# Dilation: the rows of the tiles m pitched like those of u

## The chip, the cores and the metric

The kernel runs on one core of a Trainium2 chip. The metric is the time of one execution on the device, in microseconds (us); lower is better.

## The reference

The input x is (8, 32, 256, 256) in float32. Two residual steps follow each other, each on a group-normalised x (16 groups of 2 channels):

```
x = x + dilation(_gn(x), kernel)           # 11 x 11 taps, R = 5
x = x + deformed(_gn(x), proj, dw, bn, off)   # projection, 3x3 depthwise, norm, gelu, offsets, bilinear sample

dilation: acc = -1e30
          for di, dj in 11 x 11:  acc = max(acc, pad[di:di+H, dj:dj+W] - kflat[channel, di*11+dj])
```

The change lies in the first step, the dilation: 121 taps, each a shifted copy of the image minus a constant of the channel, and the running maximum over all of them.

## The kernel before, in words

128 partitions hold 4 images x 32 channels, so there are two groups g of 128 planes. The program has four stages on one core: statistics and tables (to about 200 us), the dilation (to about 8.8 ms), the convolution and the resampling.

**Windows and chunks.** The dilation goes through each group in 16 windows of 16 output rows (WIN), and each window in 2 chunks of CR = 8 rows: 64 chunks in all. `u[s]` (two of them) is the window of x with a border of 5, 26 rows of UC = 266 elements; `dx[s]`, of the same shape, is the horizontal difference of neighbours in u, made by GpSimd (line 181). A tap pair (base, outer) needs max(u[base] - k1, u[outer] - k2), which is written as u[base] plus a relu of dx plus a constant.

**Four routes for the taps of a chunk.**

- m route, 22 pairs (`pool_pairs`): for 16 of them ScalarE writes relu(dx + gap) into `m[j % 4]` (line 591), for the other 6 (CLAMPED) GpSimd does so with a min/max (line 488). Then GpSimd adds u onto m in place (line 500; line 496 where the pair was clamped, with u as its first operand). VectorE takes acc_a = max(acc_a, m - k) (line 688; line 685 for the first of a chunk). acc_a is in PSUM.
- t route, 16 pairs (`dma_pairs`): ScalarE writes the relu into `t[j % 4]`, a DMA that GpSimd issues adds u onto t (line 471), VectorE takes the maximum (line 688). The rows of t have a pitch of 266.
- singles, 9 taps: VectorE reads u itself (line 688).
- chains: TensorE adds dx or u onto a PSUM tile (line 559), ScalarE applies a relu in place (line 609), VectorE merges a finished half chain into acc_b (line 662).

At the end of a chunk VectorE joins acc_a and acc_b (line 695) and writes x1 (line 701).

**Order.** Each engine works through an order written out by hand and repeated in every chunk. GpSimd's is `POOL_ORDER = "iitcitttcitittittcitdititcittiicttditittictitt"`: t is an add of the m route (t0 to t21), i the issue of a t-route DMA (i0 to i15), c a clamp, d a piece of dx for the next window. A writer of `m[j % 4]` waits until VectorE has used the pair four places earlier (`a_free`); four buffers are all there are.

**Layout.** `m[s]` is a tile of 8 rows of W + 4 = 260 elements (1040 bytes) of which 256 are used; the operand of u in an add is 8 rows of 256 elements at a pitch of 266 elements (1064 bytes), from row k*8 + di and column base. In the program before, tiles lie one behind the other in the on-chip memory, each at a multiple of 32 bytes: u0 begins at 23616, u1 at 51296, m0 at 139456, m1 at 147776, m2 at 156096, m3 at 164416, and the t tiles, acc_b and x1 follow them. So u0 and all m are at multiples of 64 bytes, u1 is 32 beyond one. The taps of the m route are, as (di, base): t0 (6,1), t1 (6,8), t2 (7,5), t3 (7,3), t4 (7,6), t5 (7,1), t6 (7,8), t7 (8,5), t8 (8,3), t9 (8,6), t10 (8,1), t11 (8,8), t12 (9,5), t13 (9,3), t14 (9,6), t15 (9,1), t16 (9,8), t17 (10,5), t18 (10,3), t19 (10,6), t20 (10,1), t21 (10,8).

**Other adds of GpSimd with two inputs**, which the prediction compares with: line 962, tap_a += tap_b, and line 968, h += tap_a, contiguous tiles of 4096 elements per partition, whose beginnings are 16384, 32768 or 49152 bytes apart; line 1290, dv = y[row + 1] - y[row], both operands in one tile of pitch 257; lines 1287, 1294 and 181, differences of neighbours, both operands in one tile and one element apart.

Of the kernel before, what the change touches and what calls it, by code (L numbers as in the profile page):

```python
# [15 lines left out]
P = 128  # L16
# [9 lines left out]
UR, UC = WR + 2 * R, W + 2 * R  # L26
CR = 8
# [27 lines left out]
MP, TP = 4, 4  # L55
# [57 lines left out]
def build(nc, x, params, proj_w, basis_in, mats_in, out):  # L113
# [5 lines left out]
    with ExitStack() as ctx:  # L119
# [21 lines left out]
        with ExitStack() as windows:  # L141

            u = [windows.enter_context(nc.sbuf_tensor(f"u{s}", [P, UR, UC], F32)) for s in range(2)]
            dx = [windows.enter_context(nc.sbuf_tensor(f"dx{s}", [P, UR, UC], F32)) for s in range(2)]
            outside = windows.enter_context(nc.sbuf_tensor("outside", [P, R, W], F32))
            win_loaded = [windows.enter_context(nc.semaphore(f"win_loaded{s}")) for s in range(2)]
            dx_ready = windows.enter_context(nc.semaphore("dx_ready"))
            stats_and_tables(nc, x_pl, params, basis_in, mats_in, mats, par, kt, nkt, gap_r, gap_l,
                             shift1, eps, small, pair_mean, u, dx, outside, win_loaded, dx_ready)
            dilation(nc, x_pl, x1_pl, ident, kt, nkt, gap_r, gap_l, rstd, shift1, sums1,  # L150
                     u, dx, outside, win_loaded, dx_ready)
# [182 lines left out]
def dilation(nc, x_pl, x1_pl, ident, kt, nkt, gap_r, gap_l, rstd, shift1, sums1,  # L334
# [31 lines left out]
    with ExitStack() as ctx:  # L366
        def sb(name, shape):
            return ctx.enter_context(nc.sbuf_tensor(name, shape, F32))
# [2 lines left out]
            return ctx.enter_context(nc.semaphore(name))  # L371


        m = [sb(f"m{s}", [P, CR, W + 4])[:, :, 0:W] for s in range(MP)]
        t = [sb(f"t{s}", [P, CR, UC]) for s in range(TP)]
        acc_b = sb("acc_b", [P, CR, W])
        x1 = sb("x1", [P, CR, W])
# [1070 lines left out]
```

## Time and profile before

| | |
|---|---|
| time, median of 3 | 10515.83 us (10509.91 to 10517.41) |
| the profiled execution's own time | 10515.12 us |
| its span | 10513.3 us |
| busy, of the span | VectorE 95%, GpSimd 90%, ScalarE 88%, TensorE 83% |
| DMA queue of GpSimd (q0) | 59.6% of the 16 engines |

The page of the profile gives the busy time of each engine, the span in 40 slices, and the costliest groups of instructions by line. A group's mean for GpSimd takes in the time in which an instruction lies in the engine's queue behind a DMA issue, so for its adds the distance from one start to the next says what one costs.

### The profile page before, as it was taken

Reading aid. Unit: us, or ns where it says so; the run is one execution under the profiler, and the core shown is the slowest. Engines: PE = TensorE matmul, PEld = TensorE weight load, DVE = VectorE, ACT = ScalarE, POOL = GpSimd, SP = SyncE. Lnnn points to the kernel's source line nnn. Section 1 sums busy time; section 2 is a strip of 40 time slices with the busy share of each in tenths; the row PEclk is TensorE's granted clock in tenths of the full one; section 3 lists DMA queues with packets and bytes.
Section 4 is the critical chain, followed back from the end, with each engine's and each line's share of the span. In section 5 each row is a group of like instructions: output and inputs, shape, how many; then the busy total and the mean of one; then the engine's idle time right before and its main releaser. Section 6 shows DMA issues by size and latency. Waiting matters only on the chain. (4 is left out here: it accounts for less than half of the span.)

```text
span 10513.3 us, 74673 instructions
## 1 busy us (share of the span) xinstructions
PE 8674.1 (83%) x18068; PEld 3359.2 (32%) x18068; DVE 10028.2 (95%) x5623; ACT 9204.1 (88%) x6861; POOL 9425.7 (90%) x3274
## 2 busy tenths in 40 slices
PE   2888888888888888888888888888888887888898
PEld 0333333333333333333333333333333333333333
DVE  8999999999999999999999999999999998998999
ACT  2999999999999999999999999999999996777776
POOL 2999999999999999999999999999999996666999
PEclk9999999999999999999999999999999998999999
DMA  8887878787878788888787888787888874433776
GB/s 316 156 158 152 158 149 157 149 156 152 157 154 158 155 158 155 153 157 157 155 157 154 156 156 157 154 157 155 156 157 157 156 139 130 166 155 140 267 280 252
DMA packets 442132, 1751.83 MB, mean 167 GB/s; under 512 B 23888, under 2 KB 130384, under 8 KB 392784
## 3 DMA queue, kind: packets, MB, share of 16 engines
q0 software_dynamic: 278528, 1110.51, 59.6%
q1 hardware_dynamic: 163152, 636.41, 16.0%
q8 instruction: 147, 2.41, 0.1%
q14 instruction: 305, 2.50, 0.1%
HBM read 391.58 MB, written 201.33 MB: 56 GB/s over the span
## 5 line engine op out<-in xcount | busy, mean ns | idle before, releaser
L559 PE MATMUL chain<-dx,mats 128*128 128x512 f32 x10240 | 5013.7, 635 | 971.4 <-ACT chain L609 970.3
L500 POOL TENSOR_TENSOR m<-m,u 128x2048 f32<-128x2048 f32 x1024 | 4783.9, 4835 | 21.6 <-ACT m L591 21.3
L688 DVE SCALAR_TENSOR_TENSOR acc_a<-m,kt,acc_a 128x2048 f32<-128x2048 f32 x1344 | 3162.9, 2353 | 70.7 <-POOL m L496 21.2
L559 PEld LDWEIGHTS chain<-dx,mats 128*128 128x128 f32 x10240 | 1927.3, 198 | 4057.6 <-ACT chain L609 2129.2
L609 ACT ACTIVATE chain<-chain,gap_r 128x1024 f32<-128x1024 f32 x2560 | 2696.4, 1087 | 245.4 <-PE chain L559 242.3
L688 DVE SCALAR_TENSOR_TENSOR acc_a<-t,kt,acc_a 128x2048 f32<-128x2048 f32 x1024 | 2411.9, 2355 | 34.2
L471 POOL DMA_DIRECT2D t<-u x1024 | 1621.1, 1695 | 450.6 <-ACT t L591 391.9
L496 POOL TENSOR_TENSOR m<-u,m 128x2048 f32<-128x2048 f32 x384 | 1891.1, 4925 | 0.0
L591 ACT ACTIVATE t<-dx,gap_l 128x2048 f32<-128x2048 f32 x768 | 1540.8, 2006 | 0.0
L559 PE MATMUL chain<-u,mats 128*128 128x512 f32 x3072 | 1456.0, 605 | 74.4 <-ACT chain L609 74.4
L688 DVE SCALAR_TENSOR_TENSOR acc_a<-u,kt,acc_a 128x2048 f32<-128x2048 f32 x576 | 1357.0, 2356 | 20.5
L591 ACT ACTIVATE m<-dx,gap_l 128x2048 f32<-128x2048 f32 x640 | 1281.7, 2003 | 23.2 <-DVE acc_a L688 23.2
L662 DVE SCALAR_TENSOR_TENSOR acc_b<-chain,kt,acc_b 128x1024 f32<-128x1024 f32 x768 | 965.8, 1279 | 66.2 <-PE chain L559 65.2
L559 PE MATMUL chain<-dx,neg_ident 128*128 128x512 f32 x1536 | 752.8, 627 | 330.9 <-ACT chain L609 330.9
L488 POOL TENSOR_SCALAR m<-dx,gap_l 128x2048 f32<-128x2048 f32 x384 | 966.2, 2516 | 28.3 <-DVE acc_a L688 28.2
L609 ACT ACTIVATE chain<-dx,gap_r 128x1024 f32<-128x1024 f32 x640 | 712.7, 1121 | 288.0 <-DVE acc_b L662 275.0
L559 PEld LDWEIGHTS chain<-u,mats 128*128 128x128 f32 x3072 | 547.2, 188 | 952.4 <-issue 557.2
L591 ACT ACTIVATE m<-dx,gap_r 128x2048 f32<-128x2048 f32 x384 | 766.6, 1996 | 0.0
L1054 DVE SCALAR_TENSOR_TENSOR hp<-o,par,hp 128x1024 f32<-128x1024 f32 x512 | 659.8, 1289 | 80.0 <-PE hp L868 66.5
L868 PE MATMUL hp<-o,diag 128*128 128x512 f32 x1024 | 528.5, 664 | 128.9 <-DVE h L1054 128.9
L591 ACT ACTIVATE t<-dx,gap_r 128x2048 f32<-128x2048 f32 x256 | 515.9, 2015 | 30.7 <-issue 16.4
L559 PEld LDWEIGHTS chain<-dx,neg_ident 128*128 128x128 f32 x1536 | 277.8, 194 | 805.9 <-ACT chain L609 544.4
(145 smaller groups left out, 6968.0 us busy)
## 6 DMA issues: line engine op xcount, KB each, us to landing
t<-u POOLq DMA_DIRECT2D x1024, 1059.0 KB, 8.8
u<-x_dram SPq DMA_DIRECT2D x32, 2688.0 KB, 26.7
xw<-x_scratch SPq DMA_DIRECT2D x62, 1152.0 KB, 7.3
xt<-x_dram SPq DMA_DIRECT2D x32, 2048.0 KB, 14.4
x_scratch<-x SPq DMA_DIRECT2D x64, 1024.0 KB, 11.1
h_scratch<-h SPq DMA_DIRECT2D x32, 2048.0 KB, 7.3
hw<-h_scratch SPq DMA_DIRECT2D x64, 1024.0 KB, 9.3
out_dram<-res SPq DMA_DIRECT2D x64, 1024.0 KB, 4.9
```

The lines of the kernel that those rows point to most:

```text
L471: nc.gpsimd.dma_start(t[j % TP][:].rearrange("p r w -> p (r w)")[:, 0:RUN], u[s][:].rearrange("p r w -> p (r w)")[:, first:first + RUN], a ...
L488: nc.gpsimd.tensor_scalar(m[j % MP], dx[s][:, top:top + CR, lo:lo + W], high, low, ALU.min, ALU.max).then_inc(m_clamped, 1)
L496: nc.gpsimd.tensor_tensor(m[j % MP], rows, m[j % MP], ALU.add if outer > base else ALU.subtract).then_inc(m_ready, 1)
L500: nc.gpsimd.tensor_tensor(m[j % MP], m[j % MP], rows, ALU.add).then_inc(m_ready, 1)
L559: added = nc.tensor.matmul(chain[h][:, r:r + 2, :], weight, src[:, top:top + 2, dj:dj + W], start=False, stop=True, skip_group_check=True)
L591: return nc.scalar.activation(dst, dx[s][:, k * CR + di:k * CR + di + CR, lo:lo + W], ACT.Relu, bias=gap[:, g, col(di, base):col(di, base) ...
L609: nc.scalar.activation(chain[h][:], src, ACT.Relu, bias=gap[:, g, col(di, base):col(di, base) + 1], scale=scale).then_inc(chain_relu[h], 1)
L662: nc.vector.scalar_tensor_tensor(out=part, in0=chain[h][:], scalar=kt[:, g, base:base + 1], in1=part, op0=ALU.subtract, op1=ALU.max).then_ ...
L688: nc.vector.scalar_tensor_tensor(out=acc_a[:], in0=src, scalar=k_base, in1=acc_a[:], op0=ALU.subtract, op1=ALU.max).then_inc(a_done, 1)
L868: last = nc.tensor.matmul(hp[q % 2][:, r:r + 2, :], diag[:, t, :], o[s][:, top:top + 2, tx:tx + W], start=(t == 0), stop=(t == TAPS_PE - 1))
L1054: nc.vector.scalar_tensor_tensor(out=out, in0=o[s][:, q * QR + ty:(q + 1) * QR + ty, tx:tx + W], scalar=par[:, COL_DW + t:COL_DW + t + 1], ...
```

## The change

Each m tile gets rows of UC = 266 elements in place of 260; still only the first 256 of a row are used. No instruction is added, removed or moved, and no wait changes. A tile grows from 8320 to 8512 bytes per partition, so m1, m2 and m3 begin 192, 384 and 576 bytes later, and the t tiles, acc_b, x1 and neg_ident 768 bytes later.

```
-        m = [sb(f"m{s}", [P, CR, W + 4])[:, :, 0:W] for s in range(MP)]
+        m = [sb(f"m{s}", [P, CR, UC])[:, :, 0:W] for s in range(MP)]
```

## Rows read from the trace of the kernel before

**Rows 1.** Page, part 1: busy us, share of the span, instructions of each engine

```profile
PE 8674.1 (83%) x18068; PEld 3359.2 (32%) x18068; DVE 10028.2 (95%) x5623; ACT 9204.1 (88%) x6861; POOL 9425.7 (90%) x3274
```

**Rows 2.** Busy time in 200 to 8700 us, the dilation

```profile
core 0: us, PE busy (x) PEld busy (x) DVE busy (x) ACT busy (x) POOL busy (x), PEclk, DMA share, GB/s
200.00:8700.00 8500.00, 7133.01 (x14728) 2729.63 (x14728) 8191.29 (x3930) 7898.89 (x5907) 8022.09 (x2921) 0.96 0.80 155
```

**Rows 3.** Waits of VectorE, 200 to 8700 us: total us, times, longest

```profile
DVE acc_a L685 <- issue: 72.2, 14, 5.3
DVE acc_b L662 <- PE chain L559: 64.2, 149, 5.8
DVE acc_a L688 <- POOL m L496: 20.8, 41, 1.2
DVE acc_a L685 <- POOL m L500: 20.0, 1, 20.0
DVE acc_a L688 <- POOL m L500: 19.0, 43, 0.5
```

**Rows 4.** Timeline of GpSimd over a chunk's end: start, duration, instruction, [idle before]

```profile
4346.97 1.21 POOL L471 DMA_DIRECT2D t<-u  x1 [0.44 <-issue]
4347.77 4.65 POOL L496 TENSOR_TENSOR m<-u,m 128x2048 f32<-128x2048 f32 x1
4351.94 4.61 POOL L500 TENSOR_TENSOR m<-m,u 128x2048 f32<-128x2048 f32 x1
4356.05 2.92 POOL L471 DMA_DIRECT2D t<-u  x2
4357.56 5.63 POOL L500 TENSOR_TENSOR m<-m,u 128x2048 f32<-128x2048 f32 x1
...
4365.22 5.29 POOL L496 TENSOR_TENSOR m<-u,m 128x2048 f32<-128x2048 f32 x1
4369.38 9.40 POOL L500 TENSOR_TENSOR m<-m,u 128x2048 f32<-128x2048 f32 x2
```

**Rows 5.** Timeline of VectorE over the same end

```profile
4352.54 2.36 DVE L688 SCALAR_TENSOR_TENSOR acc_a<-m,kt,acc_a 128x2048 f32<-128x2048 f32 x1 [0.44 <-POOL m L496]
...
4374.77 2.36 DVE L688 SCALAR_TENSOR_TENSOR acc_a<-m,kt,acc_a 128x2048 f32<-128x2048 f32 x1 [0.47 <-POOL m L500]
```

**Rows 6.** GpSimd's other additions and its clamp, whole run, kept apart by shape

```profile
L488 POOL TENSOR_SCALAR m<-dx,gap_l 128x2048 f32<-128x2048 f32 x384 | 966.2, 2516 | 28.3 <-DVE acc_a L688 28.2
L1290 POOL TENSOR_TENSOR dv<-y 128x2048 f32<-128x2048 f32 x64 | 291.3, 4551 | 0.0
L968 POOL TENSOR_TENSOR h<-h,tap_a 128x2048 f32<-128x2048 f32 x64 | 290.7, 4542 | 246.4 <-DVE h L1054 246.4
L962 POOL TENSOR_TENSOR tap_a<-tap_a,tap_b 128x2048 f32<-128x2048 f32 x64 | 290.7, 4542 | 121.0 <-ACT tap_b L926 121.0
L1294 POOL TENSOR_TENSOR dd<-dv 128x2048 f32<-128x2048 f32 x64 | 230.4, 3600 | 5.0
L1287 POOL TENSOR_TENSOR dh<-y 128x2048 f32<-128x2048 f32 x64 | 230.4, 3600 | 20.7 <-ACT y L1225 20.7
```

**Rows 7.** Line 688 and line 591 by tile: duration ns min/median/max, first and last start

```profile
L688 DVE SCALAR_TENSOR_TENSOR acc_a<-m,kt,acc_a x1344: 2343/2356/2358, 224.1 to 8774.0; 128x2048 f32<-128x2048 f32 x192
L688 DVE SCALAR_TENSOR_TENSOR acc_a<-t,kt,acc_a x1024: 2344/2356/2357, 228.9 to 8776.4; 128x2048 f32<-128x2048 f32 x171
L591 ACT ACTIVATE t<-dx,gap_l x768: 1988/2007/2022, 229.2 to 8753.3; 128x2048 f32<-128x2048 f32 x192
L591 ACT ACTIVATE m<-dx,gap_l x640: 1987/2002/2023, 206.2 to 8740.2; 128x2048 f32<-128x2048 f32 x160
L591 ACT ACTIVATE m<-dx,gap_r x384: 1985/1992/2023, 225.3 to 8757.2; 128x2048 f32<-128x2048 f32 x192
L591 ACT ACTIVATE t<-dx,gap_r x256: 1994/2012/2032, 198.4 to 8761.1; 128x2048 f32<-128x2048 f32 x128
```

## The prediction

> **What bounds the kernel now.** I read the page's first part, then the busy time of the dilation alone, then the waits of VectorE, and last the timelines at a chunk's end. The reader is to see that VectorE is the bound and that GpSimd stands close behind it: 95% and 90% of the span [rows 1], and in the 8500 us of the dilation 8191 and 8022 us [rows 2], with ScalarE at 7899. VectorE idles there 8500 - 8191 = 309 us. Of that only 20.8 + 19.0 = 39.8 us are waits for an add of the m route inside a chunk; 20.0 us are the one start, 72.2 us belong to loop ends and 64.2 us to TensorE's chains [rows 3]. A faster GpSimd can therefore give at most about 40 us, 0.38% of the time, and a slower one can take more.
>
> Where the 40 us lie is seen in two timelines. VectorE waits 0.44 us for the add of t20, which starts at 4347.77 and ends at 4352.42 (VectorE starts at 4352.54), and 0.47 us for t2 of the next chunk (VectorE starts at 4374.77) [rows 4, 5]. Between them GpSimd runs without a gap: the issue of i15 at 4346.97, then t20, t21, i0, i1, t0, a clamp, i2, t1, t2. So t2 comes late by whatever the five adds t20, t21, t0, t1 and t2 lose together, and t20 by what it loses itself. Each of the two waits occurs in about 42 of 64 chunks (41 and 43 times) [rows 3]; in the others the loop's end has given GpSimd a lead.
>
> **What one add costs, and on what it depends.** From start to start an add on m takes 4351.94 - 4347.77 = 4.17 us (t20), 4.11 us (t21) and 4369.38 - 4365.22 = 4.16 us (t1) [rows 4]: three taps with different rows and columns of u, the same price. GpSimd's other additions of 128x2048 fall in two classes: 4.54 and 4.55 us where the operands are far apart (lines 962, 968, 1290), and 3.60 us where they are one element apart in one tile (lines 1287, 1294) [rows 6]. The far ones have one thing in common by the layout: the distance of their operands is constant over the rows and 0 or 4 bytes beyond a multiple of 64 (16384, 32768, 49152; 1028 = 16*64 + 4). On m the distance is not constant: u's rows advance by 1064 bytes and m's by 1040, 24 bytes per row, so that the 8 rows go once through all multiples of 8 in 64 bytes. 4.13 lies at (4.13 - 3.60) / (4.55 - 3.60) = 56% of the way between the classes. My reading, an inference and not a row: two operands whose addresses agree modulo some small period get in each other's way at 4.55, others don't, and the sliding pitch of the kernel before takes the mean. That explains why all taps cost the same.
>
> **The change part by part.**
>
> - VectorE reads m at a pitch of 266 in place of 260, 1344 times at line 688. From t, which has that pitch, the same instruction has the same median, 2356 ns, as from m, and least values of 2344 and 2343 [rows 7]. Bounds: 0 and 1344 x 0.001 = 1.3 us. I take 0.
> - ScalarE writes m at 266, 1024 times. Into t it takes 2007 against 2002 ns (gap_l) and 2012 against 1992 (gap_r) [rows 7]: 640 x 0.005 + 384 x 0.020 = 10.9 us at most. ScalarE idles 8500 - 7899 = 601 us there [rows 2]. I take 0 for the end; without that cover it would be 11 us.
> - GpSimd's 384 clamps write m at 266. A clamp's mean is 2.52 us, queueing included [rows 6], and no row has one at another pitch. Bounds by the nearest pair, the two pitches in ScalarE's writes: 384 x 0.020 = 7.7 us either way, in a stretch where GpSimd idles 478 us [rows 2]. I take 0.
> - GpSimd's 1408 adds now have a constant distance over the 8 rows: 32*s + 40*di + 4*base, modulo 64 bytes, since 1064 = 16*64 + 40, a chunk (8512 = 133*64) adds nothing, and all m still begin at multiples of 64. The mean over the taps stays what it is, as the distances spread evenly over the period; a single tap goes toward 3.6 or 4.55. Bounds: 22 x (3.60 - 4.13) = -11.7 us and 22 x (4.55 - 4.13) = +9.2 us per chunk of GpSimd's time; of VectorE's, -39.8 us in all, and at most 5 x 0.42 = 2.1 us in each of 64 chunks, +134 us.
>
> What counts is then the five adds in front of t2. Modulo 32 their distances are t20 20, t21 16, t0 20, t1 16, t2 12: all are near 16, as far from 0 as the period allows, and only distances near 0 have been seen slow [rows 6]. If the period is 32 bytes (so that half of all distances are slow, as the 56% ask), these five go to nearly 3.6. t20 is 0.5 us earlier and t2 about 2 us, and both waits of VectorE go. The next one is t3, with distance 4, slow again, but behind five fast ones. I take three quarters of the 39.8 us, since ScalarE's releases and the chains (64.2 us) come next where VectorE runs earlier: -30 us. 10515.1 - 30 = 10485 us. The profiled execution, against which this is made, is 0.7 us under the median of the three runs.
>
> **A rule of the notes against this.** The Trainium skill (GPSIMD Engine Reference, Performance versus the Vector engine) gives 4497 ns for a two-input add of 2048 fp32 and calls 2.6 cycles per element the floor of two inputs that share one read port. The rows disagree with a floor: 3.60 and 4.13 us [rows 4, 6]. The same notes (SBUF — State Buffer, Specifications) give 16-byte lines with a penalty for each crossing to a new one; two far streams that take turns would then pay at any distance, also after the change. By these two rules m's adds would have no reason to stay at 4.13, and at 4.497 the bound above would be 5 x 0.37 x 64 = 118 us; that is near the third rival below.
>
> **The rivals.**
>
> 1. The period is 64 bytes. Then the five distances modulo 64 are 20, 48, 52, 16, 44 in windows with s = 0 and 52, 16, 20, 48, 12 with s = 1, all at the middle (12 to 20 from 0, of 32 at most), and the sum over the five is that of now to within one half of an add's 0.95 us. For it: two operands are slow alike at 0 and at 4 bytes, so the slow part is wide. Time: within 15 us of before, 10515.
> 2. The period is 16 bytes, or a few bytes decide. Modulo 16 the five distances are 4, 0, 4, 0, 12. If 0 and 4 are slow and 12 fast, t20 loses 0.42 us and t2 4 x 0.42 - 0.42 = 1.26 us, which VectorE waits for in 43 to 64 chunks: +54 to +81 us, about 10583. Against it: dv's distance of 4 as slow as 0, while taps with odd and even base now cost the same, which asks for an unsymmetric rule.
> 3. This ends on the other side, and most clearly: it is the constant distance itself, with the operands far apart, that is slow, at any distance, as in all the three far rows [rows 6]. GpSimd's adds go to 4.55, t2 comes 2.1 us later behind t20, t21, t0, t1; VectorE waits from the point at which GpSimd's lead (5 us after a loop's end) is used up: between 43 and 64 chunks x 2.1 = +90 to +134 us, about 10625.
> 4. The pitch does nothing: the 4.13 comes from something else, as the work beside it. Then no add moves and the time stays within 5 us, 10515. Against it: the 3.60 of dh and the 4.55 of dv stand side by side in one stretch.
>
> **How the numbers follow.** Forecast (period 32) 0.35, rival 1 0.20, rival 2 0.15, rival 3 0.12, rival 4 0.13, and 0.05 for adds that are all at 3.6, which gives -40 us. A difference within 0.2% (21 us) can't be told from no change. Faster by more than that: 0.31 of the forecast's 0.35, 0.03 of rival 1, 0.05: 0.39. Slower: rivals 2 and 3 nearly whole (0.14 + 0.12), 0.04 of rival 1 and 0.02 of the others: 0.32. The rest, 0.29, is no change. The range runs from the full 39.8 us and the small bounds (10468) to rival 2 and the lower part of rival 3 (10605). The likeliest case alone spans 10470 to 10497.
>
> **What would show it.** The start-to-start time of the adds falls apart by tap: t20, t21, t0, t1, t2 under 3.8 us, t3, t11 and t14 over 4.4. If they are half and half by the window's parity, the period is 64; if all are at 4.55, rival 3 holds. VectorE's waits for POOL m at line 688 fall from 39.8 us to under 10, or grow to over 90. The forecast is wrong if those five are not fast, or if VectorE's 40 us turn up again as waits on the chains.

## The result, and the profile after

| | us | ratio to before |
|---|---|---|
| before, median of 4 | 10516.62 (10509.91 to 10518.91) | |
| after, median of 4 | 10563.53 (10560.49 to 10573.12) | 1.0046 [1.0034, 1.0059] |

The kernel became slower by 47 us, 0.46%. I had forecast 30 us faster (10485 us, in a range of 10468 to 10605). The granted clock of TensorE is 0.957 before and 0.953 after. VectorE's waits for TensorE's chains did not grow (64.2 us [rows 3], 62.8 below), so this is not where the time went.

Where the time went is seen first in the waits of VectorE, 200 to 8750 us, of the kernel after (who waits, for whom: us in total, times, longest):

```profile
DVE acc_a L685 <- issue: 71.2, 14, 5.2
DVE acc_b L662 <- PE chain L559: 62.8, 133, 6.5
DVE acc_a L688 <- POOL m L500: 57.2, 49, 1.2
DVE acc_a L688 <- POOL m L496: 37.7, 55, 1.5
DVE acc_a L685 <- POOL m L500: 19.7, 1, 19.7
```

Against [rows 3], the waits for loop ends, for the chains and the first one are the same. Those for the adds on m grew from 39.8 to 57.2 + 37.7 = 94.9 us, by 55 us, which covers the 47 us. By tap, in the whole run, each of them is a wait for t20 (42 waits and 21.2 us before, 56 and 38.5 after) or for t2 (43 and 19.0 before, 49 and 57.2 after). But GpSimd did not get slower. Page, part 1, and the two groups of its adds, after:

```profile
PE 8713.0 (82%) x18068; PEld 3377.5 (32%) x18068; DVE 10024.5 (95%) x5623; ACT 9209.1 (87%) x6861; POOL 9380.2 (89%) x3274
...
L500 POOL TENSOR_TENSOR m<-m,u 128x2048 f32<-128x2048 f32 x1024 | 4742.9, 4765 | 83.5 <-ACT m L591 80.9
...
L496 POOL TENSOR_TENSOR m<-u,m 128x2048 f32<-128x2048 f32 x384 | 1817.5, 4733 | 0.0
```

GpSimd is busy for 9380 us where it was 9426 [rows 1], and VectorE's own work is the same to 4 us. So the sum hides the change; it is in the single adds. Timeline of GpSimd at the end of a chunk, after (start, duration, instruction; t20, t21, two DMA issues, t0, a clamp, a DMA issue, t1, t2, t3, and the clamp behind t3):

```profile
4367.07 5.01 POOL L496 TENSOR_TENSOR m<-u,m 128x2048 f32<-128x2048 f32 x1
4371.60 4.97 POOL L500 TENSOR_TENSOR m<-m,u 128x2048 f32<-128x2048 f32 x1
4376.09 2.91 POOL L471 DMA_DIRECT2D t<-u  x2
4377.61 5.25 POOL L500 TENSOR_TENSOR m<-m,u 128x2048 f32<-128x2048 f32 x1
4381.42 3.38 POOL L488 TENSOR_SCALAR m<-dx,gap_l 128x2048 f32<-128x2048 f32 x1
4383.34 2.64 POOL L471 DMA_DIRECT2D t<-u  x1
4384.89 5.66 POOL L496 TENSOR_TENSOR m<-u,m 128x2048 f32<-128x2048 f32 x1
4389.42 5.64 POOL L500 TENSOR_TENSOR m<-m,u 128x2048 f32<-128x2048 f32 x1
4393.91 4.92 POOL L500 TENSOR_TENSOR m<-m,u 128x2048 f32<-128x2048 f32 x1
4397.73 3.05 POOL L488 TENSOR_SCALAR m<-dx,gap_l 128x2048 f32<-128x2048 f32 x1
```

From start to start: t20 4.53, t21 4.49, t0 3.81, t1 4.53, t2 4.49, t3 3.82 us. In the kernel before, the same reading gives 4.11 to 4.18 [rows 4]. The durations in the second column hide this, since they begin while the instruction ahead still runs; only the starts tell. VectorE over the same end (the two instructions that take t20 and t2):

```profile
4372.20 2.35 DVE L688 SCALAR_TENSOR_TENSOR acc_a<-m,kt,acc_a 128x2048 f32<-128x2048 f32 x1 [0.38 <-POOL m L496]
...
4395.18 2.36 DVE L688 SCALAR_TENSOR_TENSOR acc_a<-m,kt,acc_a 128x2048 f32<-128x2048 f32 x1 [1.22 <-POOL m L500]
```

The first wait was 0.44 us and the second 0.47 [rows 5]. The second grew by 0.75 us, and the four adds between the two waits account for it: t21 +0.38, t0 -0.37, t1 +0.37, t2 +0.36, together 0.74. Over the dilation, all 22 adds of a chunk fall into two classes, the same in both u tiles and both chunks of a window (median from the later of the add's start and the end of the instruction ahead, 64 chunks each): 3.75 to 3.87 us for t0, t3, t5, t6, t7, t9, t10, t12, t13, t16, t17, t19, and 4.49 to 4.60 for t1, t2, t4, t8, t11, t14, t15, t18, t20, t21. Twelve are fast and ten slow, so the mean hardly moves: 4.15 us by this measure, 4.18 in the kernel before. Four of the five in front of t2, itself among them, are slow.

### The profile page after: what moved, and what is told of

It is laid out like the page before. It is cut to its first block and busy times, and to the rows that moved or that the text cites. A ratio compares the mean times of both kernels' runs of the same rounds, so it can differ in the third digit from the quotient of the medians.

```text
span 10562.0 us, 74673 instructions
## 1 busy us (share of the span) xinstructions
PE 8713.0 (82%) x18068; PEld 3377.5 (32%) x18068; DVE 10024.5 (95%) x5623; ACT 9209.1 (87%) x6861; POOL 9380.2 (89%) x3274
## 5 line engine op out<-in xcount | busy, mean ns | idle before, releaser
L688 DVE SCALAR_TENSOR_TENSOR acc_a<-m,kt,acc_a 128x2048 f32<-128x2048 f32 x1344 | 3163.0, 2353 | 126.1 <-POOL m L500 57.2
L471 POOL DMA_DIRECT2D t<-u x1024 | 1549.9, 1624 | 439.2 <-ACT t L591 414.7
L496 POOL TENSOR_TENSOR m<-u,m 128x2048 f32<-128x2048 f32 x384 | 1817.5, 4733 | 0.0
L559 PE MATMUL chain<-dx,neg_ident 128*128 128x512 f32 x1536 | 784.6, 652 | 330.8 <-ACT chain L609 330.8
L488 POOL TENSOR_SCALAR m<-dx,gap_l 128x2048 f32<-128x2048 f32 x384 | 920.4, 2397 | 72.6 <-DVE acc_a L688 72.5
```

What stands on the lines that cost most here:

```text
L471: nc.gpsimd.dma_start(t[j % TP][:].rearrange("p r w -> p (r w)")[:, 0:RUN], u[s][:].rearrange("p r w -> p (r w)")[:, first:first + RUN], a ...
L488: nc.gpsimd.tensor_scalar(m[j % MP], dx[s][:, top:top + CR, lo:lo + W], high, low, ALU.min, ALU.max).then_inc(m_clamped, 1)
L496: nc.gpsimd.tensor_tensor(m[j % MP], rows, m[j % MP], ALU.add if outer > base else ALU.subtract).then_inc(m_ready, 1)
L559: added = nc.tensor.matmul(chain[h][:, r:r + 2, :], weight, src[:, top:top + 2, dj:dj + W], start=False, stop=True, skip_group_check=True)
L688: nc.vector.scalar_tensor_tensor(out=acc_a[:], in0=src, scalar=k_base, in1=acc_a[:], op0=ALU.subtract, op1=ALU.max).then_inc(a_done, 1)
```

## The experiments

The classes fit one rule, read off this trace and so still to be tested, here **theory A**: take the address of the add's first operand minus that of its second, modulo 16 bytes; at 0 or 4 the add takes about 4.5 us, at 8 or 12 about 3.8. The sign counts, and line 496 has u first where line 500 has m first. Rows pitched 260 and 266 drift by 24 bytes, so each add had half of its rows in either class. Before the experiments it stood against **B** (rows of m off a 16-byte line, or moved tiles, cost the time) and **C** (GpSimd's whole sum sets the end, not five adds). Each ratio below is to the kernel before, timed again beside the run (10515.0 us for e1 to e4, 10515.7 for e5 to e8, 10517.8 for e9 and e10).

**e1, the m operands 8 bytes further.**

```
m = [sb(f"m{s}", [P, CR, UC])[:, :, 2:W + 2] for s in range(MP)]
```

> The change as made (pitch 266), but the 256 used elements of each m row begin at element 2, so every m operand lies 8 bytes further. Theory A (an add costs about 4.55 us where first operand's address minus second's is 0 or 4 modulo 16, about 3.8 where it is 8 or 12; VectorE is hit through the five adds t20, t21, t0, t1, t2): all 22 adds change class; t20, t21, t1, t2 become fast, t0 and t3 slow; VectorE's waits for POOL m at line 688 fall from 95 us to under 15 and the time is 10470 to 10490 us, under the kernel before. Rival B (rows of m that begin off a 16-byte line cost more, or the moved tiles do): as after the change, 10563 us, with waits of about 95 us.

Measured: 10482.92 us, ratio 0.9969 [0.9958, 0.998] to the kernel before. Timeline of GpSimd at a chunk's end in e1 (t20, t21, issues, t0 and the clamp behind it):

```profile
4334.76 4.34 POOL L496 TENSOR_TENSOR m<-u,m 128x2048 f32<-128x2048 f32 x1
4338.56 4.33 POOL L500 TENSOR_TENSOR m<-m,u 128x2048 f32<-128x2048 f32 x1
4342.32 2.99 POOL L471 DMA_DIRECT2D t<-u  x2
4344.44 5.46 POOL L500 TENSOR_TENSOR m<-m,u 128x2048 f32<-128x2048 f32 x1
4348.98 2.87 POOL L488 TENSOR_SCALAR m<-dx,gap_l 128x2048 f32<-128x2048 f32 x1
```

t20 went to 3.80, t21 to 3.76 and t0 to 4.54 us; all 22 adds changed class. Waits of VectorE for m at line 688 in e1 (the whole of them):

```profile
DVE acc_a L688 <- POOL m L496: 2.3, 4, 0.8
```

B falls: rows are as much off a 16-byte line as after the change, the tiles have moved as far, and the time is 81 us lower. Two elements turn the change into a gain.

**e2 and e3, all adds fast, all adds slow.** In both, the function `m_of(j)` takes the place of `m[j % MP]`; `m_rows` are the four tiles at a pitch of 266, and `lo` is the first element used of each row:

```
di, base, outer = pool_pairs[j]
gap = 8 * di + 4 * base if j in CLAMPED else -8 * di - 4 * base
fast = gap % 16 >= 8
lo = 0 if fast else 2            # e2; in e3: lo = 2 if fast else 0
return m_rows[j % MP][:, :, lo:lo + W]
```

> Pitch 266; each pair uses element 0 or 2 as the first of its m rows, chosen so that the distance modulo 16 is 8 or 12 in all 22 adds. Theory A: every add about 3.8 us, GpSimd's sum falls by about 22 x 0.3 = 7 us per chunk against the kernel before, VectorE's waits for POOL m nearly gone, time as in e1 within 10 us (10465 to 10485), since VectorE bounds the rest. Rival C (GpSimd's whole sum sets the end, not five adds): clearly under e1, by 20 us or more. Rival B: 10563 us.

> Pitch 266; first element 0 or 2 per pair, chosen so that the distance modulo 16 is 0 or 4 in all 22 adds. Theory A: every add about 4.55 us; t2 late by 5 x 0.4 = 2 us more than in the kernel before, where the changed kernel has 1.2; waits of VectorE for POOL m 120 to 170 us, time 10590 to 10650 us. Rival C: GpSimd's sum rises by 22 x 0.4 = 9 us per chunk, 128 of 133 us, time over 10700. Rival B: 10563 us.

Measured: e2 10477.09 us, ratio 0.9963 [0.9949, 0.9976]; e3 10627.63 us, ratio 1.0106 [1.009, 1.0121]. The adds have medians of 3.75 to 3.86 us in e2 and 4.49 to 4.59 in e3. Waits of VectorE for m, first e2, then e3 (lines 504 and 508 of these two kernels are 496 and 500, line 696 is 688):

```profile
DVE acc_a L696 <- POOL m L504: 0.9, 2, 0.5
```

```profile
DVE acc_a L696 <- POOL m L508: 99.9, 69, 2.0
DVE acc_a L696 <- POOL m L504: 59.7, 65, 1.5
```

The longest wait for t2's line is 2.0 us, five adds of 0.4. Against the 39.8 us of the kernel before, e3's waits are 99.9 + 59.7 = 159.6 us, 120 more, and its time is 113 us more. e2 lies only 6 us under e1, though e1 has 12 slow adds of 22: C is in trouble.

**e4, a pitch of 262.** `m = [sb(f"m{s}", [P, CR, 262])[:, :, 0:W] ...]`

> The kernel before with m rows pitched 262 elements, beginning at element 0. Rows of u and m then drift apart by 16 bytes per row. Theory A with a period of 16 bytes: each add keeps its class over the rows, as with 266: the same twelve adds at about 3.8, the same ten at about 4.55, time 10563 us within 10. If the period is 32 or 64 bytes or the equal pitch matters: the rows of one add differ, every add about 4.13 to 4.2, time 10516 us.

Measured: 10564.89 us, ratio 1.0046 [1.0033, 1.006]. Timeline of GpSimd in e4 (t20, t21, issues, t0, the clamp behind it):

```profile
4364.22 4.99 POOL L496 TENSOR_TENSOR m<-u,m 128x2048 f32<-128x2048 f32 x1
4368.74 4.96 POOL L500 TENSOR_TENSOR m<-m,u 128x2048 f32<-128x2048 f32 x1
4373.21 2.90 POOL L471 DMA_DIRECT2D t<-u  x2
4374.73 5.25 POOL L500 TENSOR_TENSOR m<-m,u 128x2048 f32<-128x2048 f32 x1
4378.54 3.38 POOL L488 TENSOR_SCALAR m<-dx,gap_l 128x2048 f32<-128x2048 f32 x1
```

4.52, 4.47 and 3.81 us, as with 266; the other nineteen agree too. With 16 bytes of drift per row a period of 32 or 64 would have mixed the rows. A period of 8 is out too, since 8 bytes turned every class in e1. The period is 16, and the pitches need not be equal.

**e5 and e6, only the five tight adds fast, only they slow.** As e2, with `lo = 0 if fast == (j in (20, 21, 0, 1, 2)) else 2` in e5 and `!=` in e6. The other 17 adds of a chunk are slow in e5 and fast in e6.

> Pitch 266, first element 0 or 2 per pair: the five adds t20, t21, t0, t1, t2 fast, the other 17 slow. Theory A (only the five in front of t2 hit VectorE): near e1 and e2, 10475 to 10495 us, with waits of VectorE for POOL m under 20 us, although GpSimd's sum per chunk is 17 x 0.4 - 5 x 0.35 = 5 us above the kernel before. Rival C (GpSimd's whole sum): over 10560.

> The opposite of e5: the five tight adds slow, the other 17 fast. Theory A: near e3 (10628), 10600 to 10640 us, although GpSimd's sum per chunk is 17 x 0.35 - 5 x 0.4 = 4 us under the kernel before. Rival C: 10500 or less.

Measured: e5 10496.9 us, ratio 0.9983 [0.9974, 0.9992]; e6 10594.95 us, ratio 1.0075 [1.0061, 1.0089], a little under the range I gave. Busy time in 200 to 8700 us (PE, PEld, DVE, ACT, POOL), first e5, then e6:

```profile
200.00:8700.00 8500.00, 7143.46 (x14768) 2733.20 (x14768) 8209.15 (x3939) 7917.86 (x5922) 8320.64 (x2927) 0.96 0.80 155
```

```profile
200.00:8700.00 8500.00, 7112.53 (x14588) 2725.75 (x14588) 8107.71 (x3891) 7832.45 (x5850) 7667.13 (x2893) 0.95 0.79 153
```

In the same 8500 us GpSimd works 653 us less in e6 than in e5 (90% against 98%), and e6 is 98 us slower. C falls. The other 17 adds are not quite free: making them slow costs 20 us in e5 against e2, and 33 us in e3 against e6. It is seen in VectorE's waits for m in e5, which are 22.5 us where I expected under 20 and where e2 has 0.9; 8.2 of them are for t16 and t17, the rest for t20:

```profile
DVE acc_a L696 <- POOL m L504: 14.9, 28, 0.7
DVE acc_a L696 <- POOL m L508: 7.6, 20, 1.0
```

**e7, a pitch of 264.**

> The kernel before with m rows of 264 elements: rows of u and m drift apart by 8 bytes per row, so every add alternates between a fast and a slow distance, as with 260 (24 bytes). Theory A with a period of 16: every add at 4.1 to 4.2 us, time of the kernel before within 10 us (10516). If a longer period mattered (32, 64), or the size of the tile: the taps would differ from each other or the time from 10516 by over 15 us.

Measured: 10516.64 us, ratio 1.0001 [0.9992, 1.001]. All 22 adds are at 4.12 to 4.22, and VectorE's waits for m are 44 us where the kernel before has 40. A pitch of 264 drifts by 8 bytes where 260 drifts by 24; modulo 16 that is the same.

**e8, another addition with the same trouble.** `y = [sb(f"y{s}", [P, VR + 1, W + 2])[:, :, 0:W + 1] ...]` in the resampling, on the kernel before.

> The kernel before; only in the resampling the tile y gets a pitch of 258 elements in place of 257, so that dv = y[row+1] - y[row] has its operands 1032 bytes apart (8 modulo 16) in place of 1028 (4). Theory A: dv (line 1290) falls from 4.55 to about 3.8 us, 64 x 0.75 = 48 us of GpSimd; of the time at most 48 us, and only about 10 to 20 if VectorE, nearly full there, takes over (10496 to 10506). Rival: dv's 4.55 has another cause (another row of one tile): dv stays at 4.55 and the time at 10516.

Measured: 10503.48 us, ratio 0.9987 [0.9978, 0.9996]. Line 1290 in e8 (duration ns min/median/max):

```profile
L1290 POOL TENSOR_TENSOR dv<-y x64: 3812/3817/3825, 9747.8 to 10467.2; 128x2048 f32<-128x2048 f32 x64
```

From 4551 ns [rows 6] to 3817. Of 64 x 0.73 = 47 us of GpSimd the time gives 12. VectorE is busy there for 863 of 912 us in e8, which fits, though no run isolates it. The result dv lies in a third tile, so the class hangs on the two inputs and not on where the output goes.

**e9, the operands of line 500 in the other order**, on the kernel after:

```
-   nc.gpsimd.tensor_tensor(m[j % MP], m[j % MP], rows, ALU.add)...
+   nc.gpsimd.tensor_tensor(m[j % MP], rows, m[j % MP], ALU.add)...
```

> The kernel after with the two operands of the 16 additions of line 500 in the other order (u first, m second; the sum is the same). Theory A with a sign (what counts is first minus second, and 4 is slow where 12 is fast): t0, t3, t7, t10, t13, t17 go from about 3.8 to 4.5 us, t2, t8, t15, t18 from 4.5 to 3.8; those at 0 and 8 and the six of line 496 stay. In front of t2, t20, t21, t1 and t0 are then slow and t2 fast: time near that of the kernel after, 10555 to 10575. If the sign doesn't count: no add moves.

Measured: 10557.17 us, ratio 1.0038 [1.0024, 1.0052]. Timeline of GpSimd in e9: t0 with what follows it, t2, t3:

```profile
4374.95 5.99 POOL L500 TENSOR_TENSOR m<-u,m 128x2048 f32<-128x2048 f32 x1
4379.49 3.39 POOL L488 TENSOR_SCALAR m<-dx,gap_l 128x2048 f32<-128x2048 f32 x1
...
4387.49 4.91 POOL L500 TENSOR_TENSOR m<-u,m 128x2048 f32<-128x2048 f32 x1
...
4391.26 5.63 POOL L500 TENSOR_TENSOR m<-u,m 128x2048 f32<-128x2048 f32 x1
4395.77 3.05 POOL L488 TENSOR_SCALAR m<-dx,gap_l 128x2048 f32<-128x2048 f32 x1
```

t0 went from 3.81 to 4.54, t2 from 4.49 to 3.77, t3 from 3.82 to 4.51; the ten named adds swapped, the other twelve stayed. So 4 and 12 differ, and it is first minus second that counts.

**e10, all three places.** e2 with e8's y and `tap_a = [sb(f"tap_a{s}", [P, WR * W + 2])[:, 2:].rearrange(...)]`.

> e2 (all 22 adds of a chunk at a fast distance) with y at a pitch of 258 as in e8, and with both tap_a tiles of the convolution beginning 8 bytes later, which makes the distance 8 in tap_a += tap_b and -8 in h += tap_a. Theory A: lines 962 and 968 fall from 4.54 to about 3.8 us, which the time doesn't feel, since VectorE bounds the convolution (0 to 5 us); with e2's 38 and e8's 12 us the time is about 10465 (10458 to 10470), under both kernels. If the convolution does feel it: 10450 or less.

Measured: 10461.06 us, ratio 0.9949 [0.9935, 0.9962], 0.5% under the kernel before and 1.0% under the one after. Line 970 (962 before) in e10:

```profile
L970 POOL TENSOR_TENSOR tap_a<-tap_a,tap_b x64: 3809/3814/3821, 8785.2 to 9664.8; 128x2048 f32<-128x2048 f32 x64
```

From 4542 [rows 6] to 3814 ns; line 968 (976 in e10) went from 4542 to 3809. The time doesn't show it within what can be measured: the sum of e2's 38 and e8's 12 us is 50, measured are 57 with an interval of 14 us either way.

## Why the prediction was wrong

- **What bounds the kernel: right.** VectorE bounds, it loses 39.8 us to adds, and it meets GpSimd at t20 and t2. e2 won 38 us with the waits gone, and e5 and e6 showed that the five adds up to t2 decide most of it, not GpSimd's sum: making them slow costs 79 us (e6), all 22 113 us (e3).
- **"Two operands whose addresses agree modulo some small period get in each other's way at 4.55, others don't": right in part.** The distance modulo a small period decides, the sliding pitch takes the mean (e7), and the mean over the taps stays (4.18 and 4.15). That the operands get in each other's way is shown by no run, and 12 is fast though it is as near to agreement as 4. The fast value was mis-sized too: I took 3.60 from operands one element apart, and a fast add on m takes 3.75 to 3.87. So 4.13 is not at 56% of the way but near the middle.
- **The small edits (VectorE, ScalarE, clamps): right.** After the change VectorE's busy time is 4 us less, ScalarE's 5 us more, and the clamp behind t0 takes 1.92 us from start to start in place of 1.91.
- **The step that failed is "Modulo 32 their distances are ... all near 16 ... If the period is 32 bytes ... these five go to nearly 3.6".** The period is 16 bytes (e4). Modulo 16 the same distances (u minus m, for t20, t21, t0, t1, t2) are 4, 0, 4, 0 and 12, and four of the five turned slow: t20, t21, t1, t2. So VectorE's waits grew by 55 us where I had them gone. I set the period by the 56%, which every period up to 64 meets, and gave it to the one that fitted a symmetric rule.
- **Rival 2 was the right one**, with 0.15 in place of 0.35. I held against it that it "asks for an unsymmetric rule"; the rule is unsymmetric (e9). Its price of 1.26 us for the five adds came out as (4.53 - 4.17) + (4.49 - 4.11) + (4.53 - 4.16) + (4.49 - 4.13), less (4.18 - 3.81) = 1.10 us. It had t0 slow and t2 fast, without the sign; the reverse is true, with the same sum. Its +54 to +81 us was too much, as 47 were measured: VectorE's waits grew by 55 us, and it waits for t20 in 56 and for t2 in 49 of the 64 chunks.
- **Rival 3** (any constant distance slow) falls with e1, and **rival 1** with e4. e3, where all adds are in fact slow, gives 113 us, inside rival 3's price of 90 to 134.
- **The bounds.** -39.8 us for VectorE held (e2: -38); +134 was not reached (e3: +113). The range held the result, but only by the part that was kept for rivals 2 and 3; the direction was wrong.
- **The two pages.** The Trainium skill (GPSIMD Engine Reference, Performance versus the Vector engine) has 4497 ns for such an add and explains it as the floor of two inputs. The slow adds agree with the figure (4.49 to 4.60 us), but it is no floor: e2's adds take 3.75 to 3.86 us. The Trainium skill (SBUF — State Buffer, Specifications) gives a line of 16 bytes, and the period that e4 shows is the same. Its penalty for each crossing does not explain the classes: e9 swaps only the order of the operands, each of them crosses the same lines as before, and the class changes.

## What to carry to other kernels

Before changing the pitch or place of a tile that GpSimd combines with another, compute first address minus second modulo 16 for each instruction; moving one operand by 8 bytes turned 4.5 us into 3.8 (and, where the distance was good, 3.8 into 4.5). When an engine's total stays the same but the time moves, compare its instructions start to start in the few places where the bounding engine waits for it. And if a period is only inferred from a mean, price each period that gives this mean alike, or lay the edit out so that it doesn't matter.

## What the runs showed of the hardware

- A GpSimd addition or subtraction of two float32 operands of 128x2048 in different rows or tiles took 4.49 to 4.60 us (median of each place) where first minus second was 0 or 4 modulo 16 bytes, and 3.75 to 3.87 where it was 8 or 12. This held for all 22 places of the dilation in every layout tried, in place or not (dv), and for contiguous tiles (tap_a). Distances that alternate between the two classes from row to row gave 4.12 to 4.23 (pitches 260 and 264).
- Operands one element apart in one tile are at 4 modulo 16 and take 3.60 us all the same [rows 6]. No run tells why they are faster than 8 and 12 elsewhere, or why 4 differs from 12.
- Other distances than multiples of 4 bytes, and other data types, were not tried.
